# Transposing the normed rows of a pair in one block, in two 64-row tiles of TensorE

## The chip, the core and the metric

The kernel runs on one core of a Trainium2 chip. The metric is the device time of one execution in microseconds; the kernel before takes 431.86 us (median of 3 runs, 431.16 to 431.87).

## What is computed

A cross-attention block with linear attention, and behind it a feed-forward block with ternary weights, over 8 batches of 256 rows of 512 (16 tiles of 128 rows):

```python
x = x + L0_xattn(layernorm(x), ctx, ctx, mask, ...)   # q, k, v projections; relu features; kv; out / (qk_sum + 1e-8); Wo
x = x + L0_ffn(layernorm(x), w_gate, w_up, w_down, subln_weight)
# xattn: q' = relu(q @ Wqf.T), k' = relu(k @ Wkf.T) * mask, kv = k'.T @ v, per head
# ffn:   xq = quantized rows of x; gate, up = xq @ ternary(w).T
#        a = subln(up * relu(gate)**2); y = quantized a @ ternary(w_down).T
```

The part that changes lies between the first layernorm and the query projection: the normed rows `xn` of each tile have to be transposed, so that the 512 features lie on the partitions.

## The kernel before

The program is a list of steps, each with an engine ("lane"), a planned duration, the steps it waits for and the instruction. On TensorE the steps run in the order in which the program lists them. On ScalarE (`act`), VectorE (`dve`), GpSimd (`pool`) and SyncE's queue (`sp`) a planner (`Plan.queues`, L108 to L187) sorts them: it walks through time with the durations of the table `COST` (L55 to L78) and takes in each lane the step that is due first, and among those due the one whose result TensorE needs soonest. So a changed duration or a changed order on TensorE can change the order of all other engines.

The first part of the program (L839 to L855) handles the contexts of seven batches: keys (K), values (V), the key features (`features`, F) and the 64x33 products per head (`kv`, P). What follows is written out by hand as the words of `FLOW` (L41 to L50), read by L860 to L897. A word names a block of TensorE and its arguments: V, K, P, F as above for the last batch; `L`a the layernorm of pair a (`ln1`, two tiles of 128 rows, no TensorE work); `X`i the transposes of tile i (`s1`); `W`a.h one half of the query projection of pair a (`s2`); `Q`a the query features (`s3`); `A`a the attention products (`s4`) with the division behind them on ScalarE and VectorE; `S`i the output projection of tile i, the second layernorm and the quantization of its row (`s6`); `G`i.h and `U`i.h gate and up products of tile i and half h (`gate_up`), which also list the elementwise work behind them; `D`i the down projection (`down`). Digits behind @ name PSUM banks; without them `bank` deals out banks 4 to 7 in turn.

In the names of steps, unit u = 2i + h is one half of the 2048 hidden features of a tile. For each unit ScalarE computes R, RR and zz, VectorE Z and ym; Y (the product with the subln weights) runs on VectorE if u is in `Y_ON_DVE`, else on GpSimd; yk (scaling for the quantization) on VectorE if in `YK_ON_DVE`, else on ScalarE; yb (rounding to bf16) on ScalarE if in `YB_ON_ACT`, else on VectorE. A DMA transposes the result for D.

fp32 precision comes from splitting: `hi` is a rounded copy by ScalarE, `lo` the remainder by VectorE, and products are made of three matmuls (L370). Transposes (`transposes`, L618) are fp32 matmuls against a 128x128 identity `eye`: four for a tile, 128 moving columns each, into one bank. One copy of 128x512 on ScalarE (`aph`) and one subtraction on VectorE (`apl`) empty it. The rows `xn` of a pair share one buffer, so the layernorm of pair a waits for the last transposes of pair a - 1 (L615), and W waits for both subtractions (L644). All blocks on parts of the array pass `tile_position` to the matmul: F uses 32 rows and 64 columns (L561), P all rows and 64 columns (L588), Q 32 rows and 64 columns (L660), A 64 rows and 32 columns (L683).

Most steps are issued by helpers, so the profile shows helper lines: L353 all plain matmuls, L356 ScalarE's activations, L359 elementwise of two tensors, L362 tensor with scalars, L622 the transposes, L767 the reductions ym, L794 the rounding yb.

## Time and profile before

| | before |
|---|---|
| median of 3 runs | 431.86 us (431.16 to 431.87) |
| the profiled execution | 430.77 us |
| its span, first to last instruction | 428.8 us |
| TensorE busy | 416.5 us, 97% of the span |
| TensorE weight loads busy | 287.4 us, 67% |
| VectorE busy | 343.5 us, 80% |
| ScalarE busy | 287.4 us, 67% |
| GpSimd busy | 147.4 us, 34% |
| DMA | 42.36 MB, mean 99 GB/s |

Times in the profile are microseconds from the start of the span. A matmul's length in the trace contains its way through the array, so that it overlaps the next one; what a matmul costs is read from the start of one to the start of the next. In the timeline, neighbours of one kind are merged into one row with their count, and the number in front is the start of the first. A few matmul records are missing. PE is TensorE, PEld its weight loads, DVE is VectorE, ACT ScalarE, POOL GpSimd, SP SyncE.

### The profile page before, as it was taken

Reading aid. Unit: us, or ns where it says so; the run is one execution under the profiler, and the core shown is the slowest. Engines: PE = TensorE matmul, PEld = TensorE weight load, DVE = VectorE, ACT = ScalarE, POOL = GpSimd, SP = SyncE. Lnnn points to the kernel's source line nnn. Section 1 sums busy time; section 2 is a strip of 40 time slices with the busy share of each in tenths; the row PEclk is TensorE's granted clock in tenths of the full one; section 3 lists DMA queues with packets and bytes.
Section 4 is the critical chain, followed back from the end, with each engine's and each line's share of the span. In section 5 each row is a group of like instructions: output and inputs, shape, how many; then the busy total and the mean of one; then the engine's idle time right before and its main releaser. Section 6 shows DMA issues by size and latency. Waiting matters only on the chain.

```text
span 428.8 us, 10211 instructions
## 1 busy us (share of the span) xinstructions
PE 416.5 (97%) x4292; PEld 287.4 (67%) x4323; DVE 343.5 (80%) x505; ACT 287.4 (67%) x406; POOL 147.4 (34%) x290
## 2 busy tenths in 40 slices
PE   8999999999999999999999999999999999999995
PEld 5888889889879865844774575575467566464443
DVE  4634929629969959998997897899998898998983
ACT  5675979766155177779539656865883978939970
POOL 0000000003254442383281545537225533444660
PEclk9999999999999999999999999999999999999999
DMA  7992744605502010023213033031303120423055
GB/s 231 416 416 70 261 185 164 281 2 186 209 19 103 7 26 2 12 51 87 59 48 68 0 86 75 14 74 40 63 25 62 38 49 18 84 72 64 11 120 150
DMA packets 51166, 42.36 MB, mean 99 GB/s; under 512 B 43056, under 2 KB 44080, under 8 KB 49200
## 3 DMA queue, kind: packets, MB, share of 16 engines
q1 hardware_dynamic: 51120, 41.70, 32.2%
q8 instruction: 34, 0.56, 0.5%
q14 instruction: 12, 0.10, 0.1%
HBM read 27.01 MB, written 4.19 MB: 73 GB/s over the span
## 4 chain that ended last, share of the span: by engine, by line
PE 62%; DVE 16%; ACT 6%; POOL 6%; issue 5%; DMA 4%; SPq 0%; DVEq 0%; POOLq 0%; ACTq 0%
PE ps L353 51%; DVE zb L359 3%; PE ps L588 3%; DVE rows_of L365 3%; PE ps L561 3%; PE ps L683 2%; POOL tk L362 2%; ACT rb L356 2%; PE ps L660 2%; DVE tk L767 2%; ACT kT L356 1%; POOL zb L359 1%; DMA xqT<-xqb 1%; DMA xs<-in_wk_dram 1%; DVE rows_of L359 1%
## 5 line engine op out<-in xcount | busy, mean ns | idle before, releaser
L353 PE MATMUL ps<-tg,xqT 128*128 128x512 bf16 x243 | 58.1, 379 | 2.3 <-issue 0.8
L353 PE MATMUL ps<-tu,xqT 128*128 128x512 bf16 x245 | 59.1, 379 | 1.0 <-issue 0.6
L362 POOL TENSOR_SCALAR tk<-tk 128x1 f32<-128x1 f32 x96 | 38.3, 400 | 35.8 <-DVE tk L718 18.3
L353 PE MATMUL ps<-td,yqT 128*128 128x512 bf16 x202 | 45.9, 379 | 0.5 <-issue 0.2
L353 PEld LDWEIGHTS ps<-tu,xqT 128*128 128x128 bf16 x256 | 24.2, 98 | 30.9 <-issue 2.1
L356 ACT ACTIVATE rb<-zb 128x1024 f32<-128x1024 f32 x29 | 30.6, 1056 | 20.7 <-DVE zb L359 20.5
L353 PEld LDWEIGHTS ps<-tg,xqT 128*128 128x128 bf16 x256 | 23.5, 98 | 30.8 <-issue 2.8
L359 DVE TENSOR_TENSOR zb<-ps,rb 128x1024 f32<-128x1024 f32 x29 | 35.3, 1217 | 5.6 <-ACT rb L356 5.5
L353 PE MATMUL ps<-aph,wqh 128*128 128x256 f32 x128 | 37.3, 291 | 0.0
L767 DVE TENSOR_REDUCE tk<-zb 128x1 f32<-128x1024 f32 x30 | 36.2, 1207 | 1.0 <-POOL zb L359 0.8
L353 PE MATMUL ps<-aph,wkh 128*128 128x256 f32 x128 | 36.2, 286 | 0.5 <-DVE wkl L359 0.5
L359 POOL TENSOR_TENSOR zb<-zb,g_b 128x1024 f32<-128x1024 f32 x9 | 21.7, 2412 | 42.8 <-ACT rb L356 18.6
L353 PEld LDWEIGHTS ps<-td,yqT 128*128 128x128 bf16 x208 | 19.9, 98 | 24.0 <-issue 0.7
L353 PE MATMUL ps<-apl,wqh 128*128 128x256 f32 x128 | 35.9, 280 | 0.0
L353 PE MATMUL ps<-aph,wql 128*128 128x256 f32 x128 | 35.9, 280 | 0.0
L353 PE MATMUL ps<-aph,wkl 128*128 128x256 f32 x128 | 35.3, 280 | 0.2 <-issue 0.2
L353 PE MATMUL ps<-apl,wkh 128*128 128x256 f32 x128 | 35.3, 280 | 0.1
L362 POOL TENSOR_SCALAR lnv<-mv 128x1 f32<-128x1 f32 x32 | 9.6, 300 | 72.3 <-DVE mv L607 70.3
L356 ACT ACTIVATE rb<-ps 128x1024 f32<-128x1024 f32 x29 | 29.5, 1019 | 5.0 <-PE ps L353 4.1
L356 ACT ACTIVATE rb<-rb 128x1024 f32<-128x1024 f32 x29 | 30.7, 1058 | 0.6
L359 POOL TENSOR_TENSOR xs<-xs,bo_b 128x512 f32<-128x512 f32 x16 | 22.9, 1434 | 15.0 <-DVE xn L362 10.6
L359 DVE TENSOR_TENSOR zb<-zb,g_b 128x1024 f32<-128x1024 f32 x21 | 26.0, 1242 | 2.6 <-ACT rb L356 2.6
(134 smaller groups left out, 1052.6 us busy)
## 6 DMA issues: line engine op xcount, KB each, us to landing
xs<-in_wg_dram SPq DMA_DIRECT2D x4, 1024.0 KB, 13.8
xs<-in_wu_dram SPq DMA_DIRECT2D x4, 1024.0 KB, 6.6
xs<-in_wd_dram SPq DMA_DIRECT2D x4, 1024.0 KB, 7.8
xs<-in_x_dram SPq DMA_DIRECT2D x8, 512.0 KB, 4.6
out_dram<-xs SPq DMA_DIRECT2D x15, 256.0 KB, 2.1
craw<-in_ctx_dram SPq DMA_DIRECT2D x7, 512.0 KB, 7.0
xs<-in_wk_dram SPq DMA_DIRECT2D x4, 256.0 KB, 4.4
xs<-in_wv_dram SPq DMA_DIRECT2D x4, 256.0 KB, 5.9
```

Of the source, the lines that this page charges most:

```text
L353: return add("pe", name, cost, waits, lambda e: e.matmul(out, lhsT, rhs, start=start, stop=stop))
L356: return add("act", name, cost, waits, lambda e: e.activation(out, in_, func, **kw))
L359: return add(lane, name, cost, waits, lambda e: e.tensor_tensor(out, a, b, op))
L362: return add(lane, name, cost, waits, lambda e: e.tensor_scalar(out, a, s1, s2, op0, op1))
L365: return add("dve", name, cost, waits, lambda e: e.scalar_tensor_tensor(out, a, s, b, op0, op1))
L561: add("pe", f"kf{i}.{q}.{r}.{c}", 0.015, waits, lambda e, out=out, left=left, right=right, at=(32 * r, 64 * c): e.matmul(out, left, right, ...
L588: k = add("pe", f"kv{b}.{pr}.{t}.{c}", 0.06, waits, lambda e: e.matmul(out, left, right, start=t == 0, stop=t == 1, tile_position=(0, 64 * ...
L660: add("pe", f"qf{a}.{q2}.{r}.{c}", 0.0535, waits, lambda e, out=out, left=left, right=right, at=(32 * r, 64 * c): e.matmul(out, left, righ ...
L683: add("pe", f"at{a}.{n}.{q2}.{r}.{hd}", 0.055, waits, lambda e, out=out, left=left, right=right, at=(64 * hd, 32 * r): e.matmul(out, left, ...
L767: add("dve", f"ym{u}", 1.15, [f"Y{u}"], lambda e: e.tensor_reduce(col(M0 + h, i), zs, AX_X, ALU.max, apply_absolute_value=True))
```

## The change

`X` becomes a word for a pair. `s1(a)` takes two banks and issues 16 transposes for the pair: for each of its two tiles and each of the four column groups one on the upper 64 rows and one on the lower 64 rows, against the 64x64 block of the identity that lies on the same rows. Results of the upper rows go to the first bank, those of the lower rows to the second, both tiles side by side. ScalarE's copies and VectorE's subtractions stay four for a pair, 128x512 each, but each handles the half of the rows of both tiles. The layernorm of the next pair waits for the last transposes of both halves, and W for both subtractions, as before. The planned duration of a transpose is 0.03 in place of 0.109. `FLOW` and the three lists of units are new: Y on VectorE 24 units in place of 21, yk on VectorE 18 in place of 22, yb on ScalarE 12 in place of 15.

```diff
-Y_ON_DVE = (0, 1, 2, 3, 4, 6, 8, 10, 11, 15, 16, 17, 18, 19, 21, 22, 23, 24, 26, 28, 30)
-YK_ON_DVE = (1, 3, 4, 5, 6, 8, 10, 11, 12, 14, 15, 16, 17, 18, 19, 20, 22, 23, 25, 26, 28, 30)
-YB_ON_ACT = (1, 3, 9, 13, 16, 17, 18, 19, 20, 21, 22, 25, 27, 28, 29)
+Y_ON_DVE = (0, 1, 2, 3, 4, 6, 7, 10, 11, 13, 14, 15, 16, 17, 18, 19, 21, 22, 23, 24, 26, 28, 29, 30)
+YK_ON_DVE = (0, 4, 6, 8, 10, 12, 14, 15, 17, 18, 19, 23, 25, 26, 27, 28, 30, 31)
+YB_ON_ACT = (1, 4, 7, 8, 9, 12, 17, 20, 26, 27, 28, 29)
@@
-    "X0@6 V0.4 X1@7 V4.8 V8.12 L1 V12.18 W0.0@6 W0.1@7 Q0@0123 V18.24 A0@0123 K7 P6 F7 X2@5 S0@4 P7 X3@4 S1@5 W1.0@6 W1.1@7",
-    "G0.0 Q1 U0.0 A1 G0.1 U0.1 G1.0 S2 U1.0 L2 X4 X5 G1.1 U1.1 W2.0 W2.1 S3 G2.0",
-    "U2.0 Q2 G2.1 U2.1 L3 D0 A2 G3.0 U3.0 D1 X6 G3.1 U3.1 X7 S4 S5 W3.0 D2@3 W3.1",
-    "G4.0 L4 U4.0 Q3 G4.1 U4.1 A3 G5.0 U5.0 X8 G5.1 D3 X9 S6 U5.1 S7 W4.1 D4@3 W4.0",
-    "G6.0 Q4 U6.0 G6.1 A4 U6.1 D5 G7.0 U7.0 L5 X10 S8 X11 G7.1 U7.1 S9 W5.1 D6 L6",
-    "W5.0 G8.0 Q5 U8.0 A5 G8.1 U8.1 D7 G9.0 X12 U9.0 G9.1 S10 X13 U9.1 S11 W6.0 D8@1 W6.1",
-    "G10.0 Q6 L7 U10.0 A6 G10.1 U10.1 X14 X15 G11.0 S12 U11.0 W7.0 G11.1 S13 U11.1 W7.1",
-    "G12.0 U12.0 Q7 D9@1 A7 G12.1 U12.1 D10 S14 S15 G13.0 U13.0 G13.1 U13.1 G14.0 U14.0 G14.1 U14.1 G15.0 U15.0 G15.1 U15.1 D11@3 D12 D13@0 D14@1 D15@45",
+    "X0@67 V0.4 V4.8 V8.12 L1 V12.18 W0.0@6 W0.1@7 P6 Q0@0123 V18.24 A0@0123 K7 F7 S0@4 P7 X1@74 S1@5 W1.1@7 W1.0@6",
+    "G0.0 Q1 L2 U0.0 A1 G0.1 U0.1 G1.0 S2 U1.0 X2 G1.1 U1.1 W2.1 W2.0 S3 G2.0",
+    "U2.0 Q2 G2.1 A2 U2.1 D0 G3.0 L3 X3 U3.0 G3.1 S4 U3.1 S5 D1@1 W3.0 D2 G4.0",
+    "L4 W3.1 U4.0 Q3 G4.1 A3 U4.1 D3 G5.0 U5.0 G5.1 X4 S6 S7 U5.1 W4.1 W4.0 D4@3",
+    "G6.0 Q4 U6.0 G6.1 A4 U6.1 D5 G7.0 S8 L5 X5 S9 U7.0 G7.1 U7.1 W5.0 D6 W5.1",
+    "G8.0 L6 Q5 U8.0 A5 G8.1 U8.1 D7 X6 G9.0 S10 U9.0 W6.0 G9.1 W6.1 U9.1 S11 G10.0",
+    "D8@2 Q6 U10.0 A6 L7 G10.1 U10.1 X7 G11.0 S12 U11.0 S13 G11.1 W7.0 U11.1 W7.1",
+    "G12.0 U12.0 Q7 D9@1 A7 G12.1 U12.1 D10 S14 S15 G13.0 U13.0 G13.1 U13.1 G14.0 U14.0 G14.1 U14.1 G15.0 U15.0 G15.1 U15.1 D11@3 D12@2 D13 D14@2 D15@45",
@@
-           "xT#.#": 0.109},
+           "xT#.#.#": 0.03},
@@
-        def s1(a, t):
-            i = 2 * a + t
-            b, k = transposes(f"xT{i}", xn[:, t, :], [f"xn{i}"])
-            src = ps[:, b, :].rearrange("p (a c) -> p a c", a=KC)
-            def cols(z):
-                return z[:, 0:1024].rearrange("p (a c) -> p a c", a=KC)[:, :, P * t:P * t + P]
-            act(f"xT{i}.hi", 0.5, [k], cols(aph), src, ACT.Copy)
-            bank_user[b] = [tt("dve", f"xT{i}.lo", 0.62, [k, f"xT{i}.hi"], cols(apl), src, f32(cols(aph)), ALU.subtract)]
+        def s1(a):
+            banks = [bank() for h in range(2)]
+            for t in range(2):
+                for kc in range(KC):
+                    for h in range(2):
+                        rows, o = slice(64 * h, 64 * h + 64), 128 * kc + 64 * t
+                        out, src = ps[:, banks[h], o:o + 64], xn[rows, t, P * kc:P * kc + P]
+                        waits = [f"xn{2 * a + t}", "small"] + (bank_user[banks[h]] if t == 0 else []) if kc == 0 else []
+                        add("pe", f"xT{2 * a + t}.{kc}.{h}", 0.03, waits, lambda e, out=out, src=src, rows=rows: e.transpose(out, src, eye[rows, 64 * (rows.start // 64):64 * (rows.start // 64) + 64]))
+            for h in range(2):
+                k = [f"xT{2 * a + 1}.3.{h}"]
+                src = ps[:, banks[h], :].rearrange("p (a t c) -> p a t c", a=KC, t=2)
+                def cols(z):
+                    return z[:, 0:1024].rearrange("p (a t h c) -> p h a t c", a=KC, t=2, h=2)[:, h]
+                act(f"xT{a}.{h}.hi", 0.5, k, cols(aph), src, ACT.Copy)
+                bank_user[banks[h]] = [tt("dve", f"xT{a}.{h}.lo", 0.62, k + [f"xT{a}.{h}.hi"], cols(apl), src, f32(cols(aph)), ALU.subtract)]
```

## Rows read from the trace of the kernel before

**Rows 1.** The page: busy time of TensorE, and the chain that ended last by engine.

```profile
PE 416.5 (97%) x4292; PEld 287.4 (67%) x4323; DVE 343.5 (80%) x505; ACT 287.4 (67%) x406; POOL 147.4 (34%) x290
...
PE 62%; DVE 16%; ACT 6%; POOL 6%; issue 5%; DMA 4%; SPq 0%; DVEq 0%; POOLq 0%; ACTq 0%
```

**Rows 2.** Table by stretches: stretch, length, busy us (count) per engine, clock, DMA.

```profile
152.70:406.00 253.30, 248.72 (x1834) 149.09 (x1862) 225.83 (x321) 183.68 (x266) 112.95 (x223) 1.00 0.21 47
406.00:428.80 22.80, 18.36 (x99) 9.42 (x98) 14.55 (x21) 9.56 (x12) 8.48 (x16) 1.00 0.53 128
```

**Rows 3.** The view of line 622: ns min/median/max, first and last start, shape.

```profile
L622 PE MATMUL ps<-small,xn x64: 270/272/329, 111.8 to 343.1; 128*128 128x128 f32 x64
```

**Rows 4.** TensorE's timeline (start, length, line, count): the transposes of pair 7.

```profile
342.37 1.04 PE L622 MATMUL ps<-small,xn 128*128 128x128 f32 x8
343.24 1.89 PE L353 MATMUL ps<-tg,xqT 128*128 128x512 bf16 x8
```

**Rows 5.** TensorE's timeline around P5 (L588) and F6 (L561).

```profile
105.05 0.39 PE L353 MATMUL ps<-woh,apl 128*128 128x512 f32 x1
105.37 2.06 PE L588 MATMUL ps<-vt,kp 128*64 128x33 f32 x64
107.36 0.50 PE L353 MATMUL ps<-woh,aph 128*128 128x512 f32 x1
107.69 0.39 PE L353 MATMUL ps<-wol,aph 128*128 128x512 f32 x1
107.92 0.39 PE L353 MATMUL ps<-woh,apl 128*128 128x512 f32 x1
...
110.31 1.59 PE L561 MATMUL ps<-fkr,kT 32*64 32x64 f32 x128
111.83 0.66 PE L622 MATMUL ps<-small,xn 128*128 128x128 f32 x4
```

**Rows 6.** TensorE's timeline: U2.0 and Q2.

```profile
184.78 1.89 PE L353 MATMUL ps<-tu,xqT 128*128 128x512 bf16 x8
186.60 1.12 PE L660 MATMUL ps<-qT,fkr 32*64 32x256 f32 x32
```

**Rows 7.** Timeline of the opening: Q0, P6, key copies, F7, kv copy.

```profile
122.64 1.68 PE L660 MATMUL ps<-xn,fkr 32*64 32x256 f32 x32
...
134.12 2.06 PE L588 MATMUL ps<-vt,kp 128*64 128x33 f32 x64
134.76 0.82 ACT L356 ACTIVATE kT_last<-ps,small 128x256 f32<-128x256 f32 x2
...
136.11 2.04 PE L561 MATMUL ps<-fkr,kT_last 32*64 32x64 f32 x128
...
136.26 0.28 ACT L356 ACTIVATE kvc<-ps 128x132 f32<-128x132 f32 x1 [0.50 <-PE ps L588]
```

**Rows 8.** Groups by form, 152 to 420 us: Y, yk, yb by engine.

```profile
L359 DVE TENSOR_TENSOR zb<-zb,g_b 128x1024 f32<-128x1024 f32 x21 | 26.0, 1242 | 2.6 <-ACT rb L356 2.6
L362 DVE TENSOR_SCALAR zb<-zb,tk,cm 128x1024 f32<-128x1024 f32 x22 | 18.2, 849 | 2.1 <-POOL tk L359 1.8
L794 DVE TENSOR_SCALAR yqb<-zb 128x1024 bf16<-128x1024 f32 x16 | 12.7, 816 | 0.6 <-ACT zb L356 0.4
...
L356 ACT ACTIVATE yqb<-zb,cm 128x1024 bf16<-128x1024 f32 x14 | 15.7, 1142 | 1.0 <-DVE zb L362 1.0
L356 ACT ACTIVATE zb<-zb,cm,tk 128x1024 f32<-128x1024 f32 x8 | 9.9, 1237 | 10.7 <-POOL tk L359 10.6
...
L359 POOL TENSOR_TENSOR zb<-zb,g_b 128x1024 f32<-128x1024 f32 x9 | 21.7, 2412 | 42.8 <-ACT rb L356 18.6 <-DVE qol L365 10.7 <-DVE rows_of L365 10.6
```

**Rows 9.** Timeline of the tail: yk27, Z31, D15, with idle time before.

```profile
404.80 1.23 ACT L356 ACTIVATE zbe<-zbe,cm,tk 128x1024 f32<-128x1024 f32 x1
...
409.02 1.23 DVE L359 TENSOR_TENSOR zbe<-ps,rbe 128x1024 f32<-128x1024 f32 x1 [0.35 <-ACT rbe L356]
...
422.30 3.67 PE L353 MATMUL ps<-td,yqTq 128*128 128x256 bf16 x32 [1.51 <-DMA yqTq<-yqb]
```

More of the change, by code:

```diff
@@ L61 @@
         "kT#.#.all": 0.36,  "kv#.#": 0.2, "oT#.#.hi": 0.49, "dy#.#": 0.49, "dr#.#": 0.49,
-        "qT#.#.all": 0.36, "qf#.#.rows": 0.48, "w#.#.abs": 1.91, "w#.#.fma": 1.99, "xT#.hi": 0.48, "xq#.m": 0.71,
+        "qT#.#.all": 0.36, "qf#.#.rows": 0.48, "w#.#.abs": 1.91, "w#.#.fma": 1.99, "xT#.#.hi": 0.48, "xq#.m": 0.71,
         "yk#": 1.15, "zz#": 1.05,
@@ L69 @@
         "sy#": 0.08, "v#.#.rows": 0.61, "w#.#.min": 1.14, "w#.#.tern": 0.6, "w#.mean": 0.06, "w#.scale": 0.14, "w#.sum": 0.07, "x#.#": 0.6,
-        "xT#.lo": 0.6, "xm#": 0.46, "xn#": 0.46, "xq#.b": 0.33, "y#": 0.66, "y#.#": 0.39, "yb#": 0.6, "yk#": 0.72, "ym#": 1.13,
+        "xT#.#.lo": 0.6, "xm#": 0.46, "xn#": 0.46, "xq#.b": 0.33, "y#": 0.66, "y#.#": 0.39, "yb#": 0.6, "yk#": 0.72, "ym#": 1.13,
         "zeros": 0.24,
@@ L614, in ln1 @@
                 r = ln_stats(0, i, [f"x{a}"])
-                war = [f"xT{i - 2}.3"] + ([f"oT0.{t}.hi", f"oT0.{t}.lo"] if a == 1 else []) if a else [f"warm{WARM - 1}"]
+                war = [f"xT{i - 2}.3.{h}" for h in range(2)] + ([f"oT0.{t}.hi", f"oT0.{t}.lo"] if a == 1 else []) if a else [f"warm{WARM - 1}"]
                 ts("dve", f"xn{i}", 0.34, [r, f"ln0.{i}.agg"] + war, xn[:, t, :], xs[:, i, :], mv[:, 0, i, 0:1], rstd[:, 0, i:i + 1], ALU.subtract, ALU.mult)
-        def transposes(tag, rows, waits):
-            b = bank()
-            for kc in range(KC):
-                out, src = ps[:, b, P * kc:P * kc + P], rows[:, P * kc:P * kc + P]
-                add("pe", f"{tag}.{kc}", 0.11, (waits + bank_user[b] + ["small"]) if kc == 0 else [], lambda e, out=out, src=src: e.transpose(out, src, eye))
-            return b, f"{tag}.3"
@@ L643, in s2 @@
                         if kc == 0:
-                            waits = Wq_lo + [f"xT{2 * a}.lo", f"xT{2 * a + 1}.lo"] + (bank_user[b] if oq % 2 == 0 else [])
+                            waits = Wq_lo + [f"xT{a}.{h}.lo" for h in range(2)] + (bank_user[b] if oq % 2 == 0 else [])
                         cs = slice(T * kc, T * kc + T)
@@ L893, in xattn_bitffn_kernel @@
             elif c == "X":
-                s1(n // 2, n % 2)
+                s1(n)
             elif c == "W":
```

## Prediction

> **What bounds the kernel now.** I read the page's busy shares and its chain first. TensorE is busy for 416.5 of 428.8 us, and the chain that ended last runs through it for 62% of the span, mostly in the matmul helper L353; VectorE has 16%, ScalarE and GpSimd 6% each [rows 1]. The table by stretches then tells how close the next engine is. From 152.70 to 406.00 us TensorE has 248.72 of 253.30 us busy and VectorE 225.83, which is 89%; the granted clock is 1.00, the 2.4 GHz level, there and in the tail [rows 2]. So in the stretch with six of the eight pairs' transposes every microsecond of array time counts, as long as VectorE, which is queued almost without a break, keeps up. Only in the last 22.80 us does TensorE have air (18.36 us busy).
>
> **The transposes, old form.** The view of line 622 shows 64 matmuls of 128 moving columns, each behind a 128-column load of its own [rows 3]. Eight in a row, with nothing late around them, start at 342.37 and the next matmul starts at 343.24: 0.87 us for eight, 0.109 us each [rows 4]. Removed are 64 x 0.109 = 7.0 us of TensorE time, all of it on the bound engine.
>
> **The transposes, new form.** 128 matmuls of 64 moving columns on 64 rows, alternating between the upper and the lower rows, with a 128-column load each. No row shows this form, so I bound it with the two small-tile blocks. kv uses all 128 rows and 64-column loads: 64 records from 105.37 to 107.36 are 1.99 us, 31 ns each; since no load here can share rows with another, 31 ns is the most that a 64-column load takes, and 62 ns the most for 128 columns. kf uses 32 rows and the same 64-column loads: 128 records from 110.31 to 111.83 are 1.52 us, 12 ns each [rows 5]. 12 is less than half of 31, so loads and matmuls on different row groups do run beside each other. Two row groups then give 62 / 2 = 31 ns for a record of the new form (the matmul itself, 64 of the 128 columns of a 109 ns one, is 55 ns on its tile and 27 ns with two tiles, so the load sets it). A block of 16 is 16 x 0.031 = 0.50 us. Ends: 12 ns gives 0.19 us, 62 ns gives 0.99 us. I take 31, since kf's gain from row groups is what the edit relies on.
>
> **What changing the tile shape costs.** The matmul before kv starts at 105.05 and kv at 105.37, 0.32 us, where the next untiled ones are 0.23 us apart: 0.09 us on the way in. The first two matmuls after kv are 107.36 and 107.69, 0.33 us: 0.10 us on the way out [rows 5]. Before qf, eight matmuls of 216 ns (1.73 us) take from 184.78 to 186.60, again 0.09 us on the way in [rows 6]. Every pair gets one such block, so 8 x (0.09 to 0.19). The Trainium skill (TensorEngine Tiling (Array Packing), Key Properties) says that a change of tiling mode drains the engine. The trace agrees, with 0.09 and 0.10 us; without it the sum below would be 1.0 us better. Of the 0.09 to 0.19 I take 0.12 us per block, because six of the eight blocks are followed by bf16 or fp32r matmuls whose way out I have only from the one fp32r place, and two blocks (after F6 and P7) enter from tiles already.
>
> **Sum on TensorE.** A pair costs 2 x 4 x 0.109 = 0.87 us now and 0.50 + 0.12 = 0.62 us then: 0.25 us less, 8 x 0.25 = 2.0 us less. With 12 ns it is 0.87 - 0.31 = 0.56, or 4.5 us; with 62 ns it is -0.24, or 1.9 us more.
>
> **The copies.** Two ScalarE copies and two VectorE subtractions of 128x512 per pair stay, now cut by row half and not by tile, and all wait for the last of 16 transposes. I take their length as unchanged. W needs both; the shortest cover is S1 between X1 and W1, about 3.0 us, against a latency of 0.2 and the chain copy, subtract, subtract of some 0.6 + 0.7 + 0.7 = 2.0 us. Nothing. Two banks are taken at once where it was one; the rotation gives the same total.
>
> **The opening order (F6 to W1).** P6 moves ahead of Q0, and X1 behind P7. Q0's row is 1.68 us long, that of a later qf block 1.12 us [rows 6, 7], since it comes straight behind W0 and waits for the query copies; P6 in between hides that 0.56. But P6 leaves banks 0 and 1 to ScalarE's kv copies: today F7 behind P6 takes 2.04 us, the copy at 136.26 falls inside it, and an F block without that is 1.59 long [rows 5, 7]: 0.45 us. That wait goes to Q0. F7 then stands directly behind K7, whose last key copies start at 134.76, 0.64 us after K7 gave way to P6, and take 0.82 us [rows 7]; two quarters of the features can run first, so I expect 0.6 to 0.7 us of wait there, where it has 0.45. P7 loses the cover of X2 (0.4 us) for its four VectorE feature rows. Sum: -0.56 +0.2 +0.3, near 0.
>
> **The FFN order and the split of work.** S, L, W and D1 to D6 move by a word or two against the G and U words, and each X pair now stands where one of its two words stood or near it; A2 loses U2.1 and D0 as cover for its ScalarE relus, and A3 loses U4.1. I price them at 0 +- 1.5 us. Y: 21 become 24 on VectorE, 3 x 1.24 = +3.7 us there and 3 x 2.41 = -7.2 on GpSimd. yk: 22 become 18 on VectorE, -4 x 0.85 = -3.4 there and +4 x 1.24 = +4.9 on ScalarE. yb: 15 become 12 on ScalarE, -3 x 1.14 = -3.4 there, +3 x 0.82 = +2.4 on VectorE [rows 8]. Net VectorE +2.7, ScalarE +1.5, GpSimd -7.2 us. VectorE goes from 225.8 in 253.3 to 228.5 in about 251.5, 91%: tight, not over.
>
> **The tail.** ScalarE's yk of unit 27 runs at 404.80, just ahead of the last relu; it goes to VectorE, as does Y of 29, 0.85 + 1.24 = 2.1 us of new VectorE work ahead of Z31, which starts at 409.02 after an idle of only 0.35. On the other side ScalarE is 1.24 us earlier. D15 already waits 1.51 us [rows 9]. yk31 on VectorE delays the second half of the last transfer by up to 0.8 us, behind the first eight steps of D15. From -1.0 to +1.7 us; I take 0, since the planner can put the other reductions behind Z31.
>
> **Total.** -2.0 us: span 426.8, that run 428.8. The profiled run took 430.77 us with a span of 428.8, and the median of the three runs is 431.86, so 1.1 us above it; the forecast of the median is 431.86 - 2.0 = 429.9.
>
> **Rivals.** (a) The waits are freed too: D15's 1.51 us or part of the 4.6 us between TensorE's busy time and the stretch [rows 2]. Another 1.7 us off gives 428.2. For it: GpSimd's 2.41 us Ys are among the longest steps of the chain of quantization. (b) The gain is swallowed: with VectorE at 91% TensorE arrives earlier and waits for products, relus or xq. All but 0.2 us goes: 431.7. For it: rows 2; against it: TensorE's groups show little idle now. (c) The loads of the two row groups take turns, so that a record costs 62 ns: block 0.99 + 0.12 = 1.11 us, +1.9 us, 433.8. It decides from 47 ns per record ((0.87 - 0.12) / 16), from where on the block is longer than before. Against it stands kf's 12 ns beside kv's 31. The Trainium skill (TensorE: Matmul & The Clock Gate, What happens when you issue a matmul) has a load's time scale with the column count and not with the rows; by this rule halving the rows shortens no load, and there are twice as many. The trace neither confirms nor refutes the length; what kf shows is overlap of loads, which the rule does not speak of. This is also the case in which the change doesn't do what it says. (d) VectorE is the bound: its +2.7 us reach the end and the array time doesn't matter, 434.6 less what GpSimd frees, some 433.5. It decides once VectorE's own idle in the FFN stretch (27.5 us in rows 2) cannot be used; the tail is the place where that is nearest.
>
> **How the numbers follow.** Forecast 0.42 (own range 429.0 to 430.9), (a) 0.18, (b) 0.18, (c) 0.11, (d) 0.11. The median moves by about 0.2%, 0.9 us, without meaning anything. Faster: forecast, (a) and a sliver of (b): 0.62; same: most of (b): 0.17; slower: (c), (d): 0.21. The range reaches from inside (a) to inside (c) and (d): 427.5 to 433.5.
>
> **What would show it.** The transposes' line has 128 matmuls on 64 rows, 64 moving columns each. Right: a block of 16 from its first start to the next matmul is 0.55 to 0.70 us. At 1.0 or more, (c) holds. Q0 at 1.5, F7 at 2.1 to 2.2 us. D15's wait between 0.5 and 3.2 us tells the tail. VectorE 346 us busy, GpSimd 140, ScalarE 289. If the block is 0.6 us and the span is not shorter, the waits of L353 for VectorE and ScalarE must have grown by 2 us: (b) or (d). The forecast is wrong if the re-fitted order moves TensorE's waits by more than the 2.0 us that the blocks give.

## The result and the profile after

The changed kernel is slower. Its median is 434.56 us (432.77 to 435.12, 10 runs) against 431.87 us (431.16 to 432.57, 10 runs) on the same chip, a ratio of 1.0055 with a 95% interval of 1.0042 to 1.0069. The profiled execution took 434.9 us with a span of 432.8. The ten spans of the changed kernel lie in two groups: five from 432.5 to 433.0 us, each with a mean granted clock of 0.996, and five from 430.6 to 432.3, each with 1.000. By their times, those with 0.996 are 3.0 us over before's median and those with 1.000 are 1.3 us over it. The profile shown here is from the first group, and the profile of before is 1.1 us faster than the median of its kernel, so the two profiles differ by 4.0 us where the medians differ by 2.7.

The page of the changed kernel, busy time and chain, which answer to [rows 1]:

```profile
PE 416.3 (96%) x4355; PEld 286.1 (66%) x4387; DVE 341.3 (79%) x507; ACT 289.2 (67%) x407; POOL 145.5 (34%) x287
...
PE 61%; DVE 19%; ACT 6%; issue 6%; POOL 6%; DMA 1%; DVEq 0%; POOLq 0%
```

TensorE's busy time hardly moved, since a matmul's row includes its way through the array and so overlaps the next one; VectorE has three points more of the chain. The block itself came out between the 0.55 and 0.70 us that I had named. TensorE's timeline at pair 7, where [rows 4] had 0.87 us:

```profile
346.67 0.71 PE L627 MATMUL ps<-small,xn 64*128 64x64 f32 x16
347.31 1.90 PE L353 MATMUL ps<-tg,xqT 128*128 128x512 bf16 x8
```

From 346.67 to 347.31 are 0.64 us for sixteen, 40 ns each with the way out. The eight U matmuls ahead of it take 1.82 us and not 1.73: 0.09 us for the way in. Of the eight blocks seven take 0.64 us, one 0.87 behind a wait. So a pair costs 0.73 us in place of 0.87, and eight pairs 1.1 us less.

To see where the time went I cut the span at the starts of words on TensorE, read from its timeline (us from one start to the next; D11 begins when the last U ends). The last column is the changed kernel with P6 moved back, which comes below.

| stretch | before | after | P6 back |
|---|---|---|---|
| start to X0 | 111.83 | 112.58 | 112.32 |
| X0 to F7 | 24.28 | 23.52 | 23.91 |
| F7 | 1.97 | 3.85 | 1.97 |
| S0, P7, X1, S1, W1 | 14.87 | 15.95 | 15.51 |
| G0.0 to Q2 | 33.65 | 33.53 | 33.90 |
| Q2 to Q3 | 40.64 | 39.55 | 39.54 |
| Q3 to Q4 | 34.25 | 35.65 | 35.67 |
| Q4 to Q5 | 36.01 | 35.85 | 35.85 |
| Q5 to Q6 | 36.29 | 37.51 | 37.53 |
| Q6 to Q7 | 32.39 | 32.16 | 32.15 |
| Q7 to D11 | 40.55 | 40.00 | 40.00 |
| D11 to the end | 22.1 | 22.6 | 22.6 |

A stretch without a wait is shorter by the block's 0.12 to 0.23 us (G0.0 to Q2, Q4 to Q5, Q6 to Q7). One gains more, Q2 to Q3 with 1.1. Three places lose: F7 and what follows it, Q3 to Q4, Q5 to Q6. At the end, Q7 to D11 gains 0.55 us and the rest behind it loses 0.6, so that from Q7 on the two kernels are level.

F7, which had P6 ahead of it [rows 7], now stands behind K7. The timeline of VectorE (DVE), TensorE (PE) and ScalarE (ACT) there; the bracket has the idle time before and its releaser:

```profile
132.78 3.19 DVE L365 SCALAR_TENSOR_TENSOR xn<-xn,kT 128x512 f32<-128x512 f32 x2
133.67 1.74 POOL L359 TENSOR_TENSOR xs<-xs,bo_b 128x512 f32<-128x512 f32 x1
135.89 1.28 DVE L359 TENSOR_TENSOR xn<-ps,xn 128x512 f32<-128x512 f32 x2
...
136.60 1.23 ACT L356 ACTIVATE qoh<-xn 128x512 fp32r<-128x512 f32 x2 [2.27 <-DVE xn L359]
...
138.24 1.78 PE L561 MATMUL ps<-fkr,kT_last 32*64 32x64 f32 x96 [0.58 <-ACT kT_last L356]
...
139.95 0.79 PE L353 MATMUL ps<-woh,qoh 128*128 128x512 f32 x1
...
140.54 0.63 PE L353 MATMUL ps<-wol,qoh 128*128 128x512 f32 x1
140.97 0.63 PE L353 MATMUL ps<-woh,qol 128*128 128x512 f32 x1
```

The two steps of VectorE that make the quotients of pair 0 take 3.19 us while GpSimd adds the bias (two additions, 2.99 us from 132.42). In the kernel before they had stood beside it too, but for less, and P6 hid it:

```profile
130.61 2.38 DVE L365 SCALAR_TENSOR_TENSOR xn<-xn,kT 128x512 f32<-128x512 f32 x2
```

ScalarE's queue has two copies of the quotient ahead of the last two key copies. It stands idle for 2.27 us and makes the quotient's copies first. K7's last matmul ends at 136.2, but the last two key copies start only at 137.73, and F7 waits for them. Behind that idle time S0's first matmuls start 0.59 and 0.43 us apart, and only behind 142.58 the usual 0.23. The table by stretches gives the granted clock (the number behind the busy times):

```profile
136.10:139.95 3.85, 2.84 (x130) 2.17 (x129) 3.85 (x7) 1.95 (x4) 0.00 (x0) 0.88 0.19 39
139.95:144.07 4.12, 4.12 (x17) 3.06 (x13) 2.85 (x6) 0.00 (x0) 2.75 (x2) 0.70 0.57 222
```

F7's 3.85 us are 2.84 busy, and the clock is 0.88 in it and 0.70 in S0. In narrower stretches it is 1.00 all through the wait, up to 138.6; it is at 0.50, the 1.2 GHz level, from 139.1 to 142.3, so it fell 0.8 us after F7 had gone on; and it is 1.00 again from 142.6. S0 takes 4.12 us to P7's start where the kernel before took 3.28 (138.49 to 141.77, with 0.27 of waiting).

In the FFN, TensorE's waits (line, releaser, sum, times, longest) show two transfers that were hidden in the kernel before, which in turn waited 0.23 and 0.49 us for two others:

```profile
PE ps L353 <- DMA yqT<-yqb: 1.1, 1, 1.1
...
PE ps L353 <- DMA xqT<-xqb: 1.0, 1, 1.0
```

The first is D8, the second G6.0. Ahead of G6.0 VectorE had this, again with a bias addition beside Y (252.25, 1.29 us):

```profile
252.32 2.30 DVE L359 TENSOR_TENSOR zb<-zb,g_b 128x1024 f32<-128x1024 f32 x1 [0.73 <-ACT rb L356]
254.55 0.53 DVE L362 TENSOR_SCALAR xq<-xs,mv,rstd 128x512 f32<-128x512 f32 x1
```

Y takes 2.30 us in place of 1.24 [rows 8], and the second layernorm of tile 6, which leads to xqT6, stands behind it.

The tail, answering to [rows 9]:

```profile
426.31 3.67 PE L353 MATMUL ps<-td,yqTq 128*128 128x256 bf16 x32 [1.67 <-DMA yqTq<-yqb]
```

D15's wait is 1.67 us where it was 1.51, and a wait of 0.20 us within D14 is new. All of the 0.6 us that the stretch from D11 loses lies behind the start of D13's row at 417.06; 0.36 of it are these waits, and what the rest is the profile doesn't show.

### The profile page after: what moved, and what is told of

Same layout as the page of the kernel before. It is cut to its first block, busy times and chain, and to the rows that moved or that the text cites. A ratio compares the mean times of both kernels' runs of the same rounds, so it can differ in the third digit from the quotient of the medians.

```text
span 432.8 us, 10337 instructions
## 1 busy us (share of the span) xinstructions
PE 416.3 (96%) x4355; PEld 286.1 (66%) x4387; DVE 341.3 (79%) x507; ACT 289.2 (67%) x407; POOL 145.5 (34%) x287
## 4 chain that ended last, share of the span: by engine, by line
PE 61%; DVE 19%; ACT 6%; issue 6%; POOL 6%; DMA 1%; DVEq 0%; POOLq 0%
PE ps L353 50%; DVE zb L359 6%; PE ps L588 4%; PE ps L561 3%; DVE rows_of L365 3%; DVE tk L770 3%; PE ps L686 2%; POOL tk L359 2%; ACT rb L356 2%; POOL tk L362 1%; PE ps L663 1%; ACT kT L356 1%; DVE rows_of L359 1%; DVE yqb L797 1%; DVE zb L362 1%
## 5 line engine op out<-in xcount | busy, mean ns | idle before, releaser
L362 POOL TENSOR_SCALAR tk<-tk 128x1 f32<-128x1 f32 x96 | 41.4, 431 | 42.4 <-DVE tk L721 21.4
L359 DVE TENSOR_TENSOR zb<-zb,g_b 128x1024 f32<-128x1024 f32 x24 | 30.9, 1290 | 1.5 <-ACT rb L356 1.5
L359 DVE TENSOR_TENSOR vt<-ps,bo_b 128x512 f32<-128x512 f32 x16 | 11.0, 688 | 24.7 <-PE ps L353 24.6
L353 PE MATMUL ps<-woh,qoh 128*128 128x512 f32 x64 | 27.8, 434 | 0.9 <-DVE qol L365 0.6
```

Source lines behind the costliest of these rows:

```text
L353: return add("pe", name, cost, waits, lambda e: e.matmul(out, lhsT, rhs, start=start, stop=stop))
L359: return add(lane, name, cost, waits, lambda e: e.tensor_tensor(out, a, b, op))
L362: return add(lane, name, cost, waits, lambda e: e.tensor_scalar(out, a, s1, s2, op0, op1))
```

## The experiments

Each session shares its own runs of before, so I compare distances to before: the changed kernel is 2.7 us over it. My first theory was the opening: a bare F7 behind K7. The rival was a loss spread over the new order. Two more questions ran beside: what the half rows are worth alone, and what the merging of two words into a block costs alone.

**P6 moved back.**

```diff
-    "... W0.1@7 P6 Q0@0123 V18.24 A0@0123 K7 F7 S0@4 ..."
+    "... W0.1@7 Q0@0123 V18.24 A0@0123 K7 P6 F7 S0@4 ..."
```

> The changed kernel with one word of its order moved back: P6 stands between K7 and F7 again and not ahead of Q0. Theory 1 (the loss is made in the opening: F7 stands bare behind K7 and waits for key copies that are late, TensorE idles, its granted clock falls, and S0 runs at the lower level): from the start of F7 to the start of S0 3.85 us become about 2.0, S0 4.12 about 3.2, P7 2.46 about 2.0, Q0 stays within 0.2 us; the span falls by 2 to 3 us, the median to about 431.8 (after: 434.56), and the granted clock is 1.000 in every run. Theory 2 (the loss is spread over the re-fitted order and the new block behind it): the median stays above 433.8.

Measured 433.26 us with before at 431.50 (ratio 1.0048, 1.0033 to 1.0063): 1.8 over before, so 0.9 of 2.7 us came back. F7 fell to 1.97 us as expected, and the clock was at 1.000 or 0.999 in five of the six runs; the sixth, with 0.995, took 434.51 us. But Q0 is longer again (1.61 us where the changed kernel had 1.51), and from S0's start to P7's are 3.89 us, since P7 waits:

```profile
142.08 2.06 PE L588 MATMUL ps<-vt,kp 128*64 128x33 f32 x64 [0.88 <-DVE kp L365]
```

P7 lost X2 as cover, and VectorE writes the features' rows late. So theory 1 holds for a third of the loss at most, and the two waits of the FFN stay (last column of the table).

**Matmuls to fill the wait.** Nine matmuls of 512 columns stand between K7 and F7.

```diff
-    "... K7 F7 S0@4 ..."
+    "... K7 Z9 F7 S0@4 ..."
+            elif c == "Z":
+                for z in range(n):
+                    mm(f"fill{z}", 0.216, bank_user[5] + [f"w0.{q}.tern" for q in range(4)] if z == 0 else [], ps[:, 5, :], tern[0][:, 0:128], tern[0][:, 0:512], True, True)
```

> The changed kernel with nine matmuls of 512 columns, whose result nobody reads, between K7 and F7 (9 x 0.216 = 1.94 us), so that TensorE is busy while F7's key copies are still missing. Theory 1 (part of the loss in the opening is the lower clock behind the idle time): F7 ends at about the same time as without them, but S0's matmuls start 0.23 us apart all along and not 0.43; S0 takes 3.0 us and not 4.12, the clock is 1.000 in all runs, the median is about 1.0 us below the changed kernel's slower runs, 433.5 to 434.0. Rival (the wide spacing in S0 comes from its operands, not from the clock): S0 stays at 4.1 us and the median at 434.6 or above.

```profile
135.69 2.12 PE L353 MATMUL ps<-tg 128*128 128x512 bf16 x9
137.74 1.93 PE L561 MATMUL ps<-fkr,kT_last 32*64 32x64 f32 x128
139.59 0.50 PE L353 MATMUL ps<-woh,qoh 128*128 128x512 f32 x1
139.93 0.39 PE L353 MATMUL ps<-wol,qoh 128*128 128x512 f32 x1
140.16 0.39 PE L353 MATMUL ps<-woh,qol 128*128 128x512 f32 x1
```

S0 starts at 139.59, as late behind X0 as without the fill (27.3 and 27.4 us), and its matmuls are 0.23 us apart: it was the clock, not the operands. From X0 to G0.0 this profile has 42.14 us, the changed kernel's 43.32 and before's 41.12. So in the profile the wait costs 1.0 us and the clock 1.2 more.

The median, 434.02, is 2.5 us over before (1.0044 to 1.0069), against 2.7, which that interval can't tell from nothing. But this doesn't mean that the clock costs only 0.2 us: the changed kernel's median lies between two groups that are 1.7 us apart, the five runs with the drop (0.996, 3.0 over before) and the five without (1.3 over). Against the runs with the drop the fill is 0.5 better. Among runs at full clock, P6 moved back (1.8 over) is no better than the changed kernel, so what its median gained is that the drop came in one run of six and not in five of ten. Why the fill's six runs, all at 1.000, lie 1.2 us above the changed kernel's at full clock is open: no profile of such a run of the changed kernel was taken.

**The bias additions cut.** The changed kernel and the one before, each with GpSimd's sixteen additions of the output bias on 8 of the 512 columns; the rest of the bias is left out. Orders are the same as in each uncut kernel.

```diff
-                tt("pool", f"xbo{i}", 1.23, [f"xn{i}", "bo"], xs[:, i, :], xs[:, i, :], bo_b[:, :], ALU.add)
+                tt("pool", f"xbo{i}", 1.23, [f"xn{i}", "bo"], xs[:, i, 0:8], xs[:, i, 0:8], bo_b[:, 0:8], ALU.add)
```

> The changed kernel with the sixteen GpSimd additions of the output bias cut from 512 to 8 columns (the rest of the bias is left out), the order of all engines unchanged. Theory (while GpSimd adds the bias, VectorE's operations that read two SBUF tensors take up to twice as long: the two steps ahead of F7's key copies 3.19 us for two in place of 1.3, Y beside it 1.9 to 2.3 in place of 1.24): F7's wait falls by 1.5 us or more, there is no lower clock in S0, xqT6 comes 1 us earlier; the median falls by 3 us to about 431.5. Rival (VectorE is late for its own amount of work): F7's wait and the median move by less than 0.7 us.

> The kernel before with the sixteen GpSimd additions of the output bias cut from 512 to 8 columns (the rest of the bias is left out), all orders unchanged. It gives the share of the collision with GpSimd in the difference between the kernels. With that cut the changed kernel ran at 430.4 with before at 432.4. Theory (the collision hurts the changed kernel more, since it has it ahead of F7's bare wait): before gains 1.0 to 2.0 us, to about 430.9, so the two cut kernels stand level or the changed one is up to 0.6 us faster. Rival (the collision costs both the same, the loss is elsewhere): before gains about 4 us, to 428.3.

The changed kernel falls to 430.38 us with before at 432.41 (0.9955, 0.9942 to 0.9968), the cut one of before to 430.29 with before at 432.43 (0.9951, 0.9938 to 0.9964). They stand level. The cut is worth some 4.7 us to the changed kernel (from 2.7 over to 2.0 under) and 2.1 to the one before. VectorE in the cut version of the changed kernel, at the place of the 3.19 us:

```profile
132.56 1.28 DVE L365 SCALAR_TENSOR_TENSOR xn<-xn,kT 128x512 f32<-128x512 f32 x2
```

F7 takes 2.05 us there and 3.85 with the full bias; from there to G0.0 it is 14.81 (15.95), Q3 to Q4 takes 34.58 (35.65), Q5 to Q6 36.81 (37.51). Every other stretch from X0 on is within 0.15 us of the uncut kernel's, so the whole gain lies where the changed kernel had lost. In the kernel before, Q2 to Q3 falls from 40.64 to 39.56, which is what the changed kernel has with the full bias: that was its gain of 1.1 there. So the collision sits in one stretch of the old order, besides 0.6 us between X0 and G0.0, and in three places of the new one. The same cut also frees GpSimd for its other work; what part of the gain is the collision as such wasn't separated.

**Half rows or whole rows.** Four pairs of kernels differ in the height of the transposes. In the edit below a block has eight transposes of 128 rows, each tile in its bank; the planner's table overrides the 0.109 of the call with 0.06, which is 2 x 0.03.

```diff
-                    for h in range(2):
-                        rows, o = slice(64 * h, 64 * h + 64), 128 * kc + 64 * t
...
+                    out, src = ps[:, banks[t], P * kc:P * kc + P], xn[:, t, P * kc:P * kc + P]
+                    add("pe", f"xT{2 * a + t}.{kc}", 0.109, waits, lambda e, out=out, src=src: e.transpose(out, src, eye))
```

In the first pair (the changed kernel) the plan could still shift a little; in the others the order on ScalarE, VectorE, GpSimd and SyncE is written down as lists of names and the same on both sides.

> The changed kernel with its order of words, but with the eight transposes of a pair on all 128 rows (one bank for a tile), planned at the same time in sum, so that the order on the other engines stays nearly the same. Theory 1 (the half-row form saves array time, and it reaches the end at least in part): a block takes 0.87 us in place of 0.64 (with the way in, 0.14 us more each), so 434.56 + 0.3 to 1.1 = about 435.3. Theory 2 (what the form saves is swallowed by waits, or the switching costs it): within 0.3 us of 434.56, or faster.

> As the kernel with the block alone and the other engines' order written down, but the eight transposes of a pair on all 128 rows. Against it, this shows what the half rows are worth alone. If the array time saved reaches the end: 1.1 us slower than that one, about 431.5 to 432.5. If waits elsewhere set the end: within 0.3 us of it.

> As splice, with the order on all engines kept, but the eight transposes of a pair on all 128 rows. If the 0.14 us of a pair reach the end: 0.7 to 1.1 us above splice. If waits swallow them: within 0.3 us of it.

| words around it | half rows, over before | whole rows, over before | half rows win |
|---|---|---|---|
| the changed kernel's | 2.7 | 2.8 | 0.1 |
| before's, pair 1 on banks 5 and 4 | 5.4 | 6.8 | 1.3 |
| before's, pair 1 on banks 7 and 4 | 2.4 | 4.2 | 1.8 |
| spliced (below) | 2.8 | 4.0 | 1.2 |

With the orders held, the half rows give 1.2 to 1.8 us, where TensorE's own sum says 1.1 and blocks behind a wait add to it. In the first row the win doesn't show. That pair isn't held in order, and it differs in the clock: two of six runs of the whole rows had a drop, against five of ten. At full clock the whole rows are 2.5 over before and the half rows 1.3. The profile of the whole rows has F7's wait (3.42 us for the block) and no drop behind it.

**The rows in the other order.** P6 moved back, and the block does its upper rows first.

```diff
-            for t in range(2):
-                for kc in range(KC):
-                    for h in range(2):
+            for h in range(2):
+                for t in range(2):
+                    for kc in range(KC):
```

> The kernel with P6 moved back (433.26), but the block runs its eight transposes on the upper 64 rows first and then the eight on the lower, so that no two in a row lie on different rows. If loads and matmuls on the same rows follow one another at the price that I took from kv (62 ns a record, or 55 by the matmul): a block takes 0.9 to 1.0 us in place of 0.64. If the record's price doesn't depend on the rows: 0.64 us as before. The median moves by less than 1.5 us either way.

```profile
348.75 1.01 PE L627 MATMUL ps<-small,xn 64*128 64x64 f32 x16
349.69 1.90 PE L353 MATMUL ps<-tg,xqT 128*128 128x512 bf16 x8
```

0.94 us for sixteen, 59 ns each, against 40 alternating. The bound of 62 ns from kv was near, and only the alternation makes the form pay. The median is 436.07, 3.6 over before (1.0065 to 1.0115) against 1.8: 1.9 us, for 8 x 0.30 = 2.4 us of block; the bound of 1.5 us that I had put on it was too small. Two of the four runs, the profiled one among them, had a lower clock (0.996 and 0.992); the other two are 2.7 over before, 0.9 more than with alternation, and from G0.0 to D11 the profile is only 0.5 us longer for six blocks. So much of the blocks' time went into slack.

**The block alone.** Words and lists of before; a pair's block takes the place of its second word.

```diff
-    "X0@6 V0.4 X1@7 V4.8 ... F7 X2@5 S0@4 P7 X3@4 S1@5 W1.0@6 W1.1@7",
+    "V0.4 X0@67 V4.8 ... F7 S0@4 P7 X1@54 S1@5 W1.0@6 W1.1@7",
...
-    "... D1 X6 G3.1 U3.1 X7 S4 ..."      "... X8 G5.1 D3 X9 S6 ..."
+    "... D1 G3.1 U3.1 X3 S4 ..."         "... G5.1 D3 X4 S6 ..."
```

First with a new plan for the other engines:

> The new transposes alone: order of words and lists of units as in the kernel before, with the pair's block where the second of its two words stood. Theory 1 (the block itself is worth what TensorE saves, 0.87 less 0.64 for the block and 0.09 for the way in, eight times 0.14 = 1.1 us, and only the new order loses it): about 430.8, between 430.0 and 431.4. Theory 2 (the block brings both pairs of copies late, W waits, or its use of half the rows costs something outside the block): 431.9 or more, with waits of W for VectorE's subtractions in the trace.

439.76 us with before at 431.50 (1.0168 to 1.0219), 8.3 over: far beyond both theories. G4.0 waits 4.0 us for xqT4, and Q2 to Q3 takes 46.47. To take the planner out I wrote the orders down from here on: ScalarE, VectorE, GpSimd and SyncE take their steps in a list of names from the kernel before, a pair's copies where the second tile's stood.

```diff
+        for lane, names in PIN.items():
+            out[lane] = [self.index[name] for name in names.split()]
         return out
```

> The new block alone, cleanly: words and lists of the kernel before, a pair's block in the place of its second word, and the order on ScalarE, VectorE, GpSimd and SyncE not planned anew but written down as the kernel before has it (a pair's copies both where the second tile's stood). Theory 1 (the block is good by itself, what loses is the new order around it): 8 x (0.87 - 0.64 - 0.09) = 1.1 us less on TensorE, part of it swallowed, so 430.4 to 431.4 with before at 431.5. Theory 2 (one block for two tiles makes W or the next layernorm wait): 432.5 or more, with W waiting for VectorE.

437.85 us with before at 432.41 (1.0108 to 1.0140), 5.4 over. Words, lists and banks are those of the run above, so the order that the planner had made from slightly other durations was worth 2.9 of its 8.3 us. Most of the 5.4 was mine:

```profile
149.08 0.79 PE L364 MATMUL ps<-woh,qoh 128*128 128x512 f32 x1 [2.65 <-DVE apl L370]
```

S1 on bank 5 waits for the subtraction of X1's copy from the same bank, and the clock falls behind it. With banks 7 and 4, as the changed kernel has:

> The block alone with the other engines' order written down, as in the run of that kind, but with the banks of pair 1 taken as 7 and 4, so that S1 on bank 5 doesn't wait for a subtraction of X1's (2.65 us there, and a lower clock behind it: that bank was my choice and no part of the change). Theory: the opening (end of F7 to G0) falls from 19.4 to 15.0 us, the rest stays at 1.0 us over before: median 1 to 2 us over before. Rival (a pair's block in this order makes the other engines late in the opening too): still 3 us or more over before.

> The kernel before with one change: the transposes of a pair, on 128 rows as ever, stand in one block in the place of the second word (banks 7 and 4 for pair 1), with the order on the other engines written down. Theory (merging costs, the half rows win): 3.0 to 4.2 us over before, 0.8 to 1.6 over the same with half rows (which was 2.4 over before). Rival (the merging is free, something in the half-row form costs): within 1 us of before.

The block with half rows is 434.79 us with before at 432.43 (1.0049, 1.0035 to 1.0064); with whole rows 436.41 with before at 432.22 (1.0094, 1.0079 to 1.0109). The second differs from before by the merging alone, with the first tile's copies held back to the place of the second's, and it costs 4.2 us. Its profile is that of the slowest of its six runs, with a mean clock of 0.996 and 6.9 us over before's; 2.1 of them lie ahead of F6, where nothing is changed. Its places are Q2 to Q3 (42.20 us for 40.64) and F7's end to G0.0 (17.48 for 14.87); with half rows, where the profile had a clock of 0.999, they take 41.37 and 16.21. In Q2 to Q3, G4.0 waits for xqT4. TensorE in the kernel with whole rows, then in before:

```profile
229.81 1.89 PE L364 MATMUL ps<-tg,xqT 128*128 128x512 bf16 x8 [1.13 <-DMA xqT<-xqb]
```

```profile
223.70 1.89 PE L353 MATMUL ps<-tg,xqT 128*128 128x512 bf16 x8 [0.23 <-DMA xqT<-xqb]
```

The chain that G4.0 waits for is S4, the second layernorm, the quantization and the transfer. It looks like TensorE's doing, where X6 was done ahead of G3.1 and U3.1 and its four transposes now stand directly ahead of S4. But VectorE took S4's result (the step `xs<-ps,xs`) 2.5 us and more behind the end of S4's matmuls in both kernels, so it was VectorE's queue that set the time. There, the subtraction (`apl`) of the first tile had stood ahead of the steps of yk and yb, and now both subtractions stand behind them, ahead of the layernorm. VectorE in the kernel before, then in the one with whole rows:

```profile
208.03 0.69 DVE L359 TENSOR_TENSOR apl<-ps,aph 128x512 fp32r<-128x512 f32 x1
...
211.28 1.22 DVE L359 TENSOR_TENSOR zb<-ps,rb 128x1024 f32<-128x1024 f32 x1
212.42 0.68 DVE L359 TENSOR_TENSOR apl<-ps,aph 128x512 fp32r<-128x512 f32 x1
...
214.15 0.69 DVE L359 TENSOR_TENSOR xs<-ps,xs 128x512 f32<-128x512 f32 x1
```

```profile
216.27 1.22 DVE L370 TENSOR_TENSOR zb<-ps,rb 128x1024 f32<-128x1024 f32 x1
217.41 1.28 DVE L370 TENSOR_TENSOR apl<-ps,aph 128x512 fp32r<-128x512 f32 x2
...
219.73 0.68 DVE L370 TENSOR_TENSOR xs<-ps,xs 128x512 f32<-128x512 f32 x1
```

From `zb<-ps,rb` to `xs<-ps,xs` are 3.46 us where it was 2.87: the second subtraction, 0.6 us, is in the chain.

In the opening P7 lost X2 as cover, waits 1.01 us for the feature rows, and the clock falls in the block behind it:

```profile
144.23 2.06 PE L599 MATMUL ps<-vt,kp 128*64 128x33 f32 x64 [1.01 <-DVE kp L376]
146.70 1.89 PE L636 MATMUL ps<-small,xn 128*128 128x128 f32 x8 [0.41 <-ACT kvc L367]
148.24 0.77 PE L364 MATMUL ps<-woh,qoh 128*128 128x512 f32 x1
148.81 0.63 PE L364 MATMUL ps<-wol,qoh 128*128 128x512 f32 x1
```

Then the blocks of pairs 3 to 6 in the place of the first of their words:

```diff
-    "... D1 G3.1 U3.1 X3 S4 ..."
+    "... D1 X3 G3.1 U3.1 S4 ..."
```

> Half rows and the order on the other engines written down, as in block_74, but the blocks of pairs 3 to 6 in the place of the first of their two words. Theory (the late place makes the pair's copies late for W, and moves the S or U words behind it): Q2 to Q3 falls from 41.4 to about 40.7, the median by 0.5 to 1.0 us to some 1.6 over before. Rival (the first place makes the block wait for the second tile's layernorm, or S late): no gain or slower than block_74 by up to 2 us.

435.12 us with before at 432.22 (1.0048 to 1.0074), 2.9 over against 2.4: no gain. Q2 to Q3 stays at 41.35 and Q3 to Q4 rises by 1.0, with the block now waiting 1.17 us for VectorE. S4 itself starts only 0.1 us later behind Q2 than in before, and G4.0 is still 0.7 us later: the place among TensorE's words doesn't set this cost. The two subtractions on VectorE stood where they had stood (3.46 us again), since its order was held; a kernel with them in the first tile's place wasn't run, so the late place of the copies isn't refuted.

**Attempts at a better order.** Two words moved for the two FFN waits, the other engines' order held:

```diff
-    "... G5.1 X4 S6 S7 U5.1 ..."      "D8@2 Q6 U10.0 A6 ..."
+    "... G5.1 S6 X4 S7 U5.1 ..."      "Q6 D8@2 U10.0 A6 ..."
```

> The kernel with P6 moved back, and two more words moved on TensorE alone (S6 ahead of X4; Q6 ahead of D8), with the order of all other engines kept as it was there. Theory (TensorE's waits for xqT6, 1.0 us, and yqT8, 1.1 us, are what the new order loses in the FFN, since S6 stands late and D8 early): xqT6 comes 0.6 us earlier, D8's wait falls under 0.2 us; 433.26 less 1.0 to 1.7 = 431.6 to 432.3. Rival (the transfers are late because VectorE and ScalarE are behind, and no TensorE word mends that): within 0.4 us of 433.26, the wait shows up at the next word.

436.28 us with before at 432.41 (1.0062 to 1.0117): 3.9 over, worse by 2 us than without. Q5 to Q7, so that D8 is in it on either side of Q6, takes 69.63 us where P6 moved back had 69.68: moving D8 one word on didn't free it. Q3 to Q4 takes 38.29 and not 35.67, and TensorE waits 2.1 us for an xqT in the place of the 1.0. From F7's end to G0.0 are 17.32 us for 15.51, in a profile with a mean clock of 0.992. The three runs at full clock are 2.7 over before, so more than half of the 2 us came with the clock. The rival held: the wait moved and grew.

The planner told of the collision:

```diff
-HELD = ("kk", "xn", "xm", "yb", "yk")
+HELD = ("kk", "xn", "xm", "yb", "yk", "du", "Y")
```

> The kernel with P6 moved back, with the planner told that the second step of the division (du) and Y on VectorE wait while GpSimd adds the bias or does a Y, as it is told for five other kinds; the orders on the other engines change by it, the words don't. Theory (the planner places these steps against GpSimd since it doesn't know of the collision): fewer Y at 1.9 us and more, TensorE's waits for xqT6 and yqT8 fall, 1 to 2 us less than 433.26. Rival (any change of the plan moves the waits about without sense): anywhere from 432 to 438.

434.14 us with before at 432.43 (1.0026 to 1.0060): 1.7 over, as without it. The opening behind F7 is 14.85 us for 15.51, and one wait of 2.7 us for an xqT eats it.

Then the words of the changed kernel up to tile 3 and from G10 on, those of before between, P6 moved back, the lists of units likewise:

```diff
-    "L4 W3.1 U4.0 Q3 G4.1 A3 U4.1 D3 G5.0 U5.0 G5.1 X4 S6 S7 U5.1 W4.1 W4.0 D4@3",
+    "G4.0 L4 U4.0 Q3 G4.1 U4.1 A3 G5.0 U5.0 G5.1 D3 X4 S6 U5.1 S7 W4.1 D4@3 W4.0",
```

> Half-row blocks throughout. Words and lists of units of the changed kernel for the first tiles and from G10 on, those of the kernel before for tiles 4 to 9, P6 between K7 and F7; the other engines are planned anew. Theory (the waits for xqT6 and yqT8 belong to the words chosen, not to the block): Q2 to Q3 39.6, Q3 to Q4 34.5, Q4 to Q5 36.1, Q5 to Q6 36.2, Q6 to Q7 32.2, Q7 to D11 40.0 us; 1.5 to 2 us below before, 430.3 to 431.2 with before at 432.2. Rival (the block forces them, or any new plan makes new waits): two or more of the stretches are over these by 0.8 us, the median is level with before or above.

> As splice, with the planner told that du and Y on VectorE wait for GpSimd's long operations. With P6 moved back alone, this took the opening from 15.5 to 14.9 us and gave the time away in one wait for an xqT. Expected: the opening 0.5 us shorter than splice's, the rest within 1 us of splice, either way.

> As splice, with X0 behind V0.4 and W1's halves in the order of before, so that the opening has the words of before but for the block. Expected: the opening (X0's place to G0) within 0.3 us of splice's; if the block placed later makes W0 wait, 0.5 us or more longer.

They are 434.86, 434.66 and 434.08 us with before at 432.02 (intervals 1.0054 to 1.0080, 1.0049 to 1.0073, 1.0032 to 1.0061). In the first, Q5 to Q6 is 36.04 us, under before's 36.29: with the block in place and before's words around it that stretch loses nothing, so its 1.2 us come with the new words and the plan made for them. That balance is thin: in the same kernel with whole rows, words and orders the same, the stretch takes 37.18 us, with 0.74 of waiting for a yqT. And Q3 to Q4 takes 36.78, with 1.7 us of waits (the longest 0.94 for a yqT), and Q4 to Q5 37.15, with 1.08 for S's operand qol. No complete version that I ran beats the kernel before.

## Why the prediction was wrong

**The direction.** I forecast 2.0 us less and got 2.7 more; the time lies outside my range. The sum on TensorE was right in kind and too large: I had 31 ns for a record and 0.12 us for the change of shape, 0.62 us for a pair; measured are 40 ns with the way out and 0.09 for the way in, 0.73. Eight pairs give 1.1 us and not 2.0. With orders held, 1.2 to 1.8 us reach the end. The mis-sized term is the record. The overlap of row groups, on which the term rested, is shown by the 59 and 40 ns. Rival (c) is out: in alternation the block isn't longer than before. The rule of the Trainium skill that I weighed there (TensorE: Matmul & The Clock Gate, What happens when you issue a matmul) has a load's time go by its columns. The trace agrees as far as it goes: on the same rows 59 ns for 128 columns on 64 rows, beside 31 for 64 columns on 128 rows. But my estimate for the matmul itself was 55 ns, so the 59 may be the matmul and not the load.

**The step that failed** is "The opening order", with its sum near 0, and "0 +- 1.5 us" for the FFN order. For F7 I took 0.6 to 0.7 us of wait, 2.1 to 2.2 us for the block, reading only when the last key copies run after K7; it took 3.85 (3.42 in the profile of the whole rows, at full clock). I didn't ask what stands ahead of them in ScalarE's queue, and what that waits for: two copies of a quotient that VectorE makes 3.19 us long. The profile before had the sign, the same two steps at 2.38 us, hidden behind P6. The sum itself also lost a term: I gave F7's 0.45 us of bank wait to Q0 and didn't add it there, and with it -0.56 + 0.45 + 0.2 + 0.3 is +0.4, not near 0. Q0's time I had right: from its start to the next it takes 1.51 us, 0.10 less than before. P7's lost cover is 0.88 us of waiting in the kernel with P6 back against 0.27 before, 0.6 more, where I had 0.3. The stretch from X0 to G0.0 went from 41.12 to 43.32 us, with 0.28 saved in its two blocks; 1.2 of that is the lower clock, for which the sum had no line. For the FFN order the profile has 0.5 us more from G0.0 to D11, where six blocks save 0.84: 1.3 us for the order, just inside my 1.5, but all on the losing side and not 0.

**The copies.** "Nothing", I said, with 3.0 us of cover against a latency of 2.0. W's wait indeed didn't appear in the changed kernel. But I only asked who waits for the copies, and not what they push back in VectorE's queue (the layernorm behind S4 and its chain to the next gate), nor who loses the block as cover (P7). The kernel with the merging alone, in the old order, is 4.2 us over before, and my sum had no line for it. What the merging costs inside the changed kernel, with its own order, wasn't measured; its Q2 to Q3, where the old order lost 1.6 us, is 1.1 shorter than before's.

**The split of work.** Net VectorE +2.7 us: the page has 341.3 after 343.5, so the total was no guide. Rival (d), that VectorE's added work reaches the end, isn't what the stretches show: those without a wait got shorter. VectorE does count by its place: its part of the chain rose from 16% to 19%. Y on VectorE is slower by place, not by count: 1.29 us in the mean after 1.24, with single ones at 2.30 and 1.92. Rival (b), waits for VectorE and ScalarE in the place of what TensorE saved, was the right kind, but I had it end level. What makes it worse than level is shown by the cut bias: without the long GpSimd additions both kernels stand level at 430.3 and 430.4. Even then the 1.1 us that the blocks save doesn't show.

**The tail** moved by +0.16 us in D15's wait, and by 0.6 us from D11 to the end, within my -1.0 to +1.7.

**The balance.** From the kernels with before's order held: merging +4.2, half rows -1.8, together +2.4. The changed kernel with its own words and lists stands at +2.7, and at full clock the two are 1.4 and 1.3 over. So the new order as a whole, taken against the old with the same block, brought nothing that can be measured. Against before it wins 1.1 us in Q2 to Q3 and 0.55 in Q7 to D11, and gives that back at F7, G6.0, D8 and in the tail. This account and that of the cut bias look at the same 2.7 us from two sides and can't be added; the merging wasn't run with the bias cut. Which part of the merging's 4.2 us lies at which word is shown only for the two places above: single profiles differ by up to 2.1 us ahead of F6 alone, where all kernels do the same.

## What to carry to other kernels

When an edit joins two small steps of the bound engine, price where its followers now stand in the queues of the other engines and what used to be covered by the part that moved, not only who waits for its result; here that cost 4.2 us with the old order, more than the array time saved. Before a cover is taken from an in-order queue, read that queue in the trace: the wait is set by the entry ahead of the one you need, with its worst length and not its mean. And where a planner orders other engines from planned durations, compare edits with those orders written down, or the new plan is part of what you measure (2.9 us here). Where runs fall into groups by their granted clock, compare the groups too: a median between two groups moves when only their share does.

## What the runs showed of the hardware

Row tiles of fp32 transposes overlap only in alternation: 128-column loads with 64 moving columns cost 40 ns a record alternating between two row groups (way out included) and 59 ns on the same rows, against 109 ns for a full one.

A VectorE operation with two inputs in SBUF stands still while GpSimd adds two SBUF tensors: two steps of 0.69 us took 3.19 us together, a Y of 1.22 took 2.30, and with GpSimd's addition cut to 8 columns the two took 1.28. Two steps with one input in PSUM took 1.29 beside the same kind of addition (before, from 129.40). The Trainium skill (SBUF — State Buffer, Who interferes with whom) says that such an operation and a GpSimd operation that reads SBUF lock each other out for a whole instruction; the trace agrees, with these numbers.

F7 with 1.0 us of idle time in three pieces was followed by the 1.2 GHz level in the profile of the changed kernel, 0.8 us after TensorE had gone on: S0's first matmuls start up to 0.59 us apart and then 0.43, until 142.25. The profile of the whole rows has nearly the same pieces of idle time in F7 and no drop, and by their mean clock five of the ten runs of the changed kernel had none either. So nearly the same wait was followed by the drop in one profile and not in another; what decides it isn't shown. P6 moved back, without idle time in F7, had a lower mean clock in one run of six.

The first thirteen matmuls, the same in all kernels, last from 1.24 to the next start at 5.72 in before's profile, at 6.17 in the changed kernel's and at 6.95 in that of the merging alone, all at a granted clock of 1.00. Up to the start of F6 the profiles differ by 2.1 us (110.31, 111.06 and 112.40). So a single profile of this kernel carries up to 2 us that have nothing to do with an edit.
